# The end of a 16-tile binary-convolution and attention kernel, put in another order

## What is computed

```python
def _L0(x):                                   # v = _gn(x)
    out = bconv3x3(tile(v, 4), w1, groups=4)  # sign of input and of weights
    out = relu(batchnorm(out))
    out = batchnorm(bconv3x3(out, w2, groups=4))
    out = sum over 4 parallel groups of lambda * out
    return relu(out + v)
def _L1(x):                                   # v = _gn(x)
    m = bilinear resize of masks to 28x28
    mid = v * m
    atten = sigmoid(conv7x7([mean_c(mid), max_c(mid), m]))
    out = mid * atten
    rn = instance norm of out, with gamma and beta
    return relu(5 * rn)
x = x + _L0(_gn(x));  x = x + _L1(_gn(x))
```

## Time and profile before

| | us |
|---|---|
| median of 3 runs | 228.22 (227.88 to 228.31) |
| the profiled execution, its own time | 227.68 |
| its span, first to last instruction | 225.9 |
| busy PE, DVE, ACT, POOL | 198.2, 152.0, 173.8, 154.3 |

### The profile page before, as it was taken

One profiled execution on the slowest core, in us unless ns is written; L12 is line 12 of the kernel. 1 busy time (PEld: TensorE's weight loads), 2 busy tenths in 40 slices (PEclk: granted clock), 3 DMA queues, 4 the chain that ended last, 5 costly groups with the idle time before them and its releaser, 6 DMA issues.

```text
span 225.9 us, 8997 instructions
## 1 busy us (share of the span) xinstructions
PE 198.2 (88%) x3807; PEld 123.7 (55%) x3807; DVE 152.0 (67%) x440; ACT 173.8 (77%) x230; POOL 154.3 (68%) x216
## 2 busy tenths in 40 slices
PE   8998997999899989889998998899999998698810
PEld 3456554465566566546564665466556655366710
DVE  2676365965846887677686854775657565988874
ACT  2785889888769878798899878989899888341392
POOL 8532273727142996799769978797879877947960
PEclk9999999999999999999999999999999999999965
DMA  6998004642217040744073404431453236124117
GB/s 199 334 299 303 15 4 112 198 141 68 81 61 231 3 145 7 228 131 145 3 207 86 147 1 151 141 97 52 121 173 73 75 97 193 64 84 144 74 71 284
DMA packets 12429, 28.48 MB, mean 126 GB/s; under 512 B 2293, under 2 KB 4213, under 8 KB 12389
## 3 DMA queue, kind: packets, MB, share of 16 engines
q1 hardware_dynamic: 11653, 26.84, 38.5%
q10 hardware_dynamic: 736, 1.06, 1.5%
HBM read 21.29 MB, written 6.61 MB: 124 GB/s over the span
## 4 chain that ended last, share of the span: by engine, by line
PE 41%; POOL 19%; ACT 12%; DVE 11%; issue 9%; DMA 4%; SPq 1%; ACTq 1%; POOLq 0%; DVEq 0%
PE c L1025 10%; PE c L1004 10%; PE small L1082 6%; POOL X L437 6%; PE small L1070 5%; POOL o L432 3%; ACT S L599 3%; DMA att_b<-attention_rows 3%; ACT acc L622 3%; DVE RD L799 2%; POOL o L419 2%; DVE bnst L740 2%; ACT word L584 2%; PE y L1045 2%; DMA o<-in_w 2%
## 5 line engine op out<-in xcount | busy, mean ns | idle before, releaser
L1025 PE MATMUL c<-S,w2t 64*32 64x392 f16 x2304 | 55.1, 331 | 7.9 <-DVE RD L799 7.3
L1004 PE MATMUL c<-E,w1t 64*128 64x420 f16 (+1 forms) x576 | 54.5, 330 | 0.9 <-ACT E L578 0.7
L799 DVE SCALAR_TENSOR_TENSOR RD<-RD,c 128x784 f16<-128x784 f16 x32 | 30.8, 964 | 29.5 <-ACT RD L606 29.4
L1025 PEld LDWEIGHTS c<-S,w2t 64*32 64x32 f16 x2304 | 31.8, 92 | 26.9 <-issue 14.0
L1004 PEld LDWEIGHTS c<-E,w1t 64*128 64x128 f16 x576 | 25.5, 94 | 25.2 <-issue 7.7
L740 DVE BATCH_NORM_STATS2 bnst<-X 128x6 f32<-128x392 f32 x64 | 32.6, 552 | 6.1 <-POOL X L437 3.3
L584 ACT ACTIVATE word<-c 128x840 int32<-128x840 f32 (+1 forms) x32 | 26.0, 812 | 9.3 <-PE c L1004 9.3
L419 POOL TENSOR_TENSOR o<-o,mask_b 128x784 f32<-128x784 f32 x14 | 26.1, 1868 | 9.2 <-ACT o L628 9.2
L594 ACT ACTIVATE S<-word,thr_high 128x840 f16<-128x840 int16 (+1 forms) x32 | 30.4, 951 | 0.6
L437 POOL TENSOR_TENSOR X<-X,acc 128x784 f32<-128x784 f32 x14 | 26.0, 1856 | 6.3 <-ACT acc L622 6.3
L599 ACT ACTIVATE S<-word,thr_low_act 128x840 f16<-128x840 uint16 (+1 forms) x32 | 30.0, 937 | 0.0
(11 more groups left out here) (135 smaller groups left out, 266.6 us busy)
## 6 DMA issues: line engine op xcount, KB each, us to landing
X<-in_x SPq DMA_DIRECT2D x16, 392.0 KB, 6.1
mask_b<-mask_rows SPq DMA_DIRECT2D x32, 196.0 KB, 3.5
out<-o SPq DMA_DIRECT2D x15, 392.0 KB, 3.9
att_b<-attention_rows SPq DMA_DIRECT2D x28, 196.0 KB, 4.6
o<-in_w ACTq DMA_DIRECT2D x1, 576.0 KB, 5.2
o<-in_masks SPq DMA_DIRECT2D x1, 512.0 KB, 8.9
band<-in_band SPq DMA_DIRECT2D x1, 441.0 KB, 10.1
cs<-in_cst SPq DMA_DIRECT2D x1, 434.0 KB, 6.2
```

The lines of the kernel that those rows point to most:

```text
L799: dve.scalar_tensor_tensor(RD[:, hh, 1, :], RD[:, hh, 0, :], -IMG / TINY, second_sums(t, hh), ALU.mult, ALU.add).then_inc(low2, 1)
L1004: mm = pe.matmul(c1[:, 512 - n * (1 - i):512 + n * i], w1t[64 * i:64 * i + 64, s, :], window(START[i][hh], ROWS[hh], s, E[64 * i:64 * i + ...
L1025: mm = pe.matmul(second_bank(t, hh)[at:at + Q32, LOW + HALF * i:LOW + HALF * (i + 1)], w2t[64 * r:64 * r + 64, s, q, :], window(RH * half_ ...
```

## The change

- The last half of the second convolution, `conv2(15, 1)`, is cast on ACT ahead of `relu_block(14)`, subtracted on DVE ahead of `add_last(14)`, and mixed on PE directly behind `mix(15, 0)`, ahead of the turns of tile 13.
- x1 of tile 15 is added on POOL (`add_x(15)`, behind `attend(11)`), no longer on DVE; that of tile 14 stays on DVE.
- `stats_o(10)` goes from its place ahead of `add_last(14)` to one behind the last `reduce_chunks`. With it `scale3(10)`, the last relu and the last sum of tile 10 move: the power and the sum on POOL behind `attend(13)`, the relu into ACT's last run, and the three columns of tile 10 from POOL to ACT (POOL_SCALES is 10).
- `finish_block(15)` stands ahead of the reductions of tile 13, and both `stats_x1(14)` and `stats_x1(15)` ahead of `terms2(14)`.
- The last sum of tile 12 goes from DVE to POOL (POOL_SUMS is 13), behind `scale3(15)`.

```diff
--- before.py
+++ after.py
@@ -282,9 +282,9 @@
             return next(n for n, (a, z) in enumerate(BATCHES) if a <= t < z)
 
         POOL_ATTENDS = NT - 2
-        POOL_SUMS = NT - 4
+        POOL_SUMS = NT - 3
         POOL_X = NT - 2
-        POOL_SCALES = NT - 5
+        POOL_SCALES = NT - 6
 
         LAST_TURNS = [(NT - 2, 0), (NT - 2, 1), (NT - 1, 0), (NT - 2, 2), (NT - 1, 1), (NT - 1, 2)]
 
@@ -373,7 +373,7 @@
             for t in range(NT - 6, NT - 1):
                 store_out(t)
             for h in range(2):
-                sp.wait_ge(fin_last, 4 + h)
+                sp.wait_ge(fin_last, 3 + h)
                 part_of = slice(HALF * h, HALF * (h + 1))
                 sp.dma_start(out_v[NT - 1, :, part_of], o[:, NT - 1, part_of]).then_inc(stored, 16)
             sp.wait_ge(stored, (NT + 1) * 16)
@@ -432,7 +432,7 @@
                     pool.tensor_tensor(o[:, t, :], o[:, t, :], att_b[:, t % 2, :], ALU.mult).then_inc(o_ready, 1)
 
             def add_x(t):
-                if has(t) and t < POOL_X:
+                if has(t) and t != NT - 2:
                     pool.wait_ge(block_relu, t + 1)
                     pool.tensor_tensor(X[:, t, :], X[:, t, :], acc0[:, t % 2, :], ALU.add).then_inc(x1_ready, 1)
 
@@ -549,21 +549,22 @@
 
             make_u(NT - 3)
             mask_column(NT - 3)
-            scale3(NT - 6)
             attend(NT - 5)
+            add_x(NT - 1)
             power2(NT - 2)
             power2(NT - 1)
             mask_column(NT - 2)
             mask_column(NT - 1)
-            last_sum(NT - 6)
             attend(NT - 4)
             attend(NT - 3)
-            scale3(NT - 5)
-            scale3(NT - 4)
+            for t in range(NT - 6, NT - 3):
+                scale3(t)
+            last_sum(NT - 6)
             scale3(NT - 3)
             last_sum(NT - 5)
             scale3(NT - 2)
             scale3(NT - 1)
+            last_sum(NT - 4)
 
 
         @block.scalar
@@ -720,15 +721,14 @@
                 normalise2(k - 2)
                 sigmoid(k - 3)
 
+            high_sums(NT - 1, 1)
             relu_block(NT - 2)
-            high_sums(NT - 1, 1)
-            last_relu(NT - 6)
             relu_block(NT - 1)
             sigmoid(NT - 3)
             diagonal(NT - 2)
             diagonal(NT - 1)
             sigmoid(NT - 1)
-            for t in range(NT - 5, NT - 1):
+            for t in range(NT - 6, NT - 1):
                 late_relu(t)
             late_relu_halves(NT - 1)
 
@@ -748,10 +748,10 @@
 
             def stats_x1(t):
                 if has(t):
-                    if t < POOL_X:
-                        dve.wait_ge(x1_ready, t + 1)
+                    if t == NT - 2:
+                        dve.wait_ge(x1_last, 1)
                     else:
-                        dve.wait_ge(x1_last, t - POOL_X + 1)
+                        dve.wait_ge(x1_ready, min(t + 1, NT - 1))
                     stats_of(t, 1, X[:, t, :])
 
             def stats_o(t):
@@ -934,22 +934,21 @@
                 low_sums(k, 0)
                 finish_block(k - 1)
 
-            stats_o(NT - 6)
+            low_sums(NT - 1, 1)
             add_last(NT - 2)
-            low_sums(NT - 1, 1)
+            finish_block(NT - 1)
             reduce_chunks(NT - 3, 0)
             reduce_chunks(NT - 3, 1)
-            finish_block(NT - 1)
+            stats_x1(NT - 2)
             reduce_chunks(NT - 3, 2)
-            stats_x1(NT - 2)
-            add_last(NT - 1)
+            stats_x1(NT - 1)
             terms2(NT - 2)
-            stats_x1(NT - 1)
             u_of_last(NT - 2)
             terms2(NT - 1)
             u_of_last(NT - 1)
             for t, n in LAST_TURNS:
                 reduce_chunks(t, n)
+            stats_o(NT - 6)
             stats_o(NT - 5)
             stats_o(NT - 4)
             stats_o(NT - 3)
@@ -958,7 +957,7 @@
             attend_last(NT - 1)
             stats_o(NT - 1)
             dve.wait_ge(rstd3, NT)
-            for t in range(NT - 4, NT - 1):
+            for t in range(NT - 3, NT - 1):
                 last_sum(t)
             last_sum_halves(NT - 1)
 
@@ -1185,9 +1184,9 @@
 
             conv2(NT - 1, 1)
             mix(NT - 1, 0)
+            mix(NT - 1, 1)
             turn(NT - 3, 0)
             turn(NT - 3, 1)
-            mix(NT - 1, 1)
             turn(NT - 3, 2)
             keep_clock(4, c2)
             attention(NT - 3)
```

## The result

The changed kernel takes **230.27 us** (median of 4 runs, 229.61 to 230.84) where the kernel before, run beside it, takes 228.26 (227.88 to 228.35): a ratio of **1.0093, interval 1.007 to 1.0117**, 2.0 us slower. The prediction was 230.4, slower. The profiled run of after is the longest of its four, 230.84 with a span of 229.0; that of before was shorter than its median. So the two traces stand 3.2 us apart where the medians stand 2.0 apart, and a part of the gap between them is not the change's.

The account below looks back on a forecast made before the run. Bound after the loop by PE's attention of tile 13 with fillers, then DVE's last sums and halves: end +2.2 us, including front +0.2, takes 227.68 to 229.9 profiled, 230.4 us on the median; range 229.2 to 231.6.

Parts of the forecast that it names:

- The end: Last sums and halves on DVE: they end at 224.9 instead of 222.70, +2.2 us with the front's 0.2 within it.
- The list of sums and powers on POOL: POOL after tile 12's power: two sums and three powers take 6.25 us, so tile 15's power ends 1.4 us later.
- The exclusion of POOL's and DVE's last sums: After tile 15's power: POOL's sum of tile 12 goes first and DVE waits, ending at 224.9 instead of about 224.1.
- rival 1: Last sums: DVE gets in first, the store of tile 12 waits until 223.2, total 231.4 us; chance 0.13.
- Rival 2: Last sums: POOL and DVE share SBUF after all, ACT's relus decide, total 229.4 us; chance 0.14.
- The front: DVE and PE: attention of tile 13 and fillers 0.3 us later, of which slack takes 0.1, leaving +0.2 us.
- x1 of tile 15: Its sum on POOL: statistics ready 2.3 us earlier, counted as nothing because fillers hold the matmul until 204.24.
- The start of POOL's list: POOL at the end: tile 12's power follows DVE's statistics and ends at 214.1, with no wait for ACT.
- Tile 10's old sum: POOL's sum of tile 10 before the change: lay in idle time, so taking it away brings nothing.
- The fillers cover: PE ahead of tile 15's matmul: fillers cover both the slower POOL sum and the 2.3 us gained, until 204.24.
- Rival 3: Tile 15's statistics, not fillers, hold its matmul: 2.3 us gained pays for the end, 228.0 us; chance 0.12.
- rival 4: PE idles longer ahead of tile 13's attention, the granted clock falls and 4.80 us doubles, total 235 us; chance 0.03.

Follow-up runs that it names:

- b_sum12_pool: The kernel before with only the last sum of tile 12 moved to POOL, behind its last power: 228.76 us, ratio 1.0025.
- a_few_fillers: The changed kernel with 2 instead of 14 filler matmuls ahead of the small matmul of tile 15: 230.23 us, ratio 1.0081.
- a_piece13_first: The changed kernel with the last piece of tile 13's maxima ahead of the statistics of tile 14 on DVE: 229.51 us, ratio 1.0064.
- v1_tile10_late: v1 plus tile 10's move (statistics, power, relu, columns, sum) as in the change: 228.23 us, ratio to before 0.9999.
- v1: The kernel before with the last half first, tile 13's maxima ahead of tile 15's block end, tile 10's relu behind tile 13's sigmoid: 227.19 us, ratio 0.9970.
- a_tile10_back: The changed kernel with tile 10's statistic, power, relu and sum back at the front, not quite in the old order: 230.42 us, ratio 1.0101.
- a_tile10_clock: a_tile10_back plus four filler matmuls between the last two mixes on PE: 230.47 us, ratio to before 1.0112.
- b_front: a_tile10_clock with the last sum of tile 12 on DVE again, leaving only the change's front: 228.90 us, ratio to before 1.0031.

## Why the prediction was right, and which steps were off

**The end was right in its mechanism and nearly in size.** The list of sums and powers on POOL was put at 6.25 us; from the sum of tile 10 at 215.07 to the end of the last power at 221.35 it took 6.28. The exclusion of POOL's and DVE's last sums was put at 0.8 (224.9 against 224.1) and measured 0.74 in after and 0.75 in b_sum12_pool (223.35 - 218.87 less 3.73); that POOL goes first, and not DVE (rival 1), is seen from POOL's sum, which starts at 221.31 and takes its usual 1.84, against the 3.49 us of DVE's two. Rival 2, sums side by side, falls with the 3.49 us of b_sum12_pool. The Trainium skill, "SBUF — State Buffer", section "Who interferes with whom", states that exclusion; the rows of before had shown it only for a sum against other work, b_sum12_pool shows it for a sum against a sum.

**The front was right in its start and wrong in its way to the end.** The attention of tile 13 starts 0.28 us later, forecast 0.3. The prediction let that reach the end through the fillers and DVE, as 0.2; but a_few_fillers shows slack on that way, and a_piece13_first that the end follows the attention by way of its rows and that this order is worth 0.76 us to the whole. x1 of tile 15 gains 2 us that nothing takes up.

**The start of POOL's list was argued from the wrong wait.** The prediction let the powers follow DVE's statistics of tile 12 and so put the end of tile 12's power at 214.1, 0.5 earlier than the third power of before (214.57), with no wait for ACT. It had 214.83, and the relu then held POOL for 0.24 more: the list began at 215.07, with 0.40 of that the run's own lateness, so 0.6 later than forecast. Between stands the way of the attention rows, which the prediction left out: POOL's attends waited 1.41 us for their load, and the powers followed these.

**Tile 10's old sum was free only in part.** The prediction said that it lay in idle time and that taking it away brings nothing. Before, SP's loads of the rows for POOL's attend of tile 12 (issues, their start, time to landing):

```profile
L330 SPq DMA_DIRECT2D att_b<-attention_rows x2: 491/542/592, 203.3 to 203.8; - x2
DMA to landing us min/median/max: 3.3/3.4/3.5
```

So these rows were there at about 203.8 + 3.5 = 207.3, in the middle of the sum (206.57 to 208.41): some 0.7 us of it lay in the wait for them, and the rest held the attends up by about 1.0 us. After the change this 1.0 was gained and lost again: the run's lateness (0.40), the front (0.28) and a load that landed 8.7 us behind the attention's start instead of 8.2 bring the attends 0.26 us later than before. And the same 1.84 us stand again ahead of the powers. In v1_tile10_late the attends come 0.92 us sooner behind the attention than in v1, but one sum and one power make POOL's list 2.65 us longer (215.74 - 213.09), of which 0.54 replaces v1's wait for DVE.

**"The fillers cover" was true and beside the point.** Rival 3 held that if the fillers let the matmul of tile 15 come 2.3 us sooner, it could pay for the end. a_few_fillers let it come 1.45 sooner, and the time stayed: after the change that path has slack. The prediction had warned that POOL's end would not follow in full; it did not follow at all. (Rival 3's own sum takes off the front's 0.2 twice, since it lies within the 2.2: it should give 228.2.)

**The clock** (rival 4) stayed at 1.00 in after from 186 to 216, as in the row of 196 to 199. That it was near is seen in a_tile10_back.

By the traces, measured from the attend of tile 10, the change cost 34.00 - 31.28 = 2.7 us (DVE's end), by the medians 2.0 with an interval of about 1.6 to 2.7; the forecast of 2.2 lies between. That the number came out within 0.2 is in part luck, two misses of opposite sign: the list started late, which the prediction missed, and the runs of after lie 0.6 below its profiled one, which it could not know.

## What to carry over

Look for the longest chain that still has to run when the loop ends, here the attention of tile 13 with its rows stored and loaded again, and pull forward what starts it; a statistic that is early but waits for fillers gains nothing. An operation that lies in another one's wait is free only there, and only as far as the wait reaches: moved into a list that an in-order engine works through ahead of what others wait for, it makes that list longer by its whole length. Before an engine is relieved by another, see from a row that the two really run side by side.

## What the hardware showed beyond that

- Behind 1.39 us without a matmul the granted clock was 0.50 for the stretch 196 to 199 of a_tile10_back; a wait of 1.02 us ahead of a mix at 193.73 in after left it at 1.00. In a_tile10_clock it fell at 214 to 218 while PE was busy throughout. The same 32 matmuls of the spread took 3.79 us in eight of the thirteen traces and 3.98 to 5.39 in the other five; what brings that on stays open.
- The store and reload of the attention rows takes 1.92 and 3.99 us in the chain of after, and 8.82 us pass from the attention's first matmul to the attend that uses it. In the seven traces in which that attend waits for the load it is 8.31 to 8.82 us, but 10.19 in b_front: a load of the same size varies from run to run by more than some of the prices here.
- POOL's power of tile 14, 0.55 us alone, took 1.27 beside DVE's product in after, like that of tile 15 before.
